# One more buffer in each ring of a scan unit, and two of its inputs made a unit earlier

## What is computed

```python
x = L0(x)   # layernorm, two state-space scans (one over the reversed sequence), gate, residual
x = L1(x)   # layernorm, token gather, conv, one state-space scan, gate, residual
x = L2(x)   # softmax attention, 16 heads
x = L3(x)   # linear attention, 8 heads
```

```python
delta = softplus(dlt @ Wdt.T + bdt)
dA  = exp(delta[..., None] * A)                     # B, S, E, N
dBu = delta[..., None] * Bm[:, :, None, :] * u[..., None]
h = dA_t * h + dBu_t                                # step by step over the 256 tokens
y = einsum('ben,bn->be', h, C_t)
```

## Time and profile before

| what | us |
|---|---|
| median of 3 runs | 3707.52 |
| lowest, highest | 3702.73, 3718.88 |
| span of the profiled execution | 3709.0 |

### The profile page before, as it was taken

How to read it: one execution, slowest core, us unless ns; L and a number is a source line. 1 busy time by engine, 2 the same in 40 slices (tenths; PEclk the granted TensorE clock), 3 DMA queues, 4 the chain that set the end, 5 groups by cost and what they waited for, 6 DMA issues and landing times.

```text
span 3709.0 us, 64650 instructions
## 1 busy us (share of the span) xinstructions
PE 3242.9 (87%) x22078; PEld 2674.0 (72%) x22078; DVE 2851.3 (77%) x3590; ACT 2921.7 (79%) x6624; POOL 2833.8 (76%) x3087
## 2 busy tenths in 40 slices
PE   6677788899999999999999999899989999897876
PEld 2556667787777878787877778787877777675643
DVE  1568778889797979798887979798888979793621
ACT  1658878888889898888888898988988898873522
POOL 0578989888898889888888888888888889780500
PEclk8899999999999999999999999999999999997866
DMA  4112222222122222212221222212221222220100
GB/s 170 59 51 82 80 66 65 85 65 88 61 87 63 83 63 80 74 59 89 65 87 58 82 69 79 71 60 89 63 88 60 87 61 78 60 69 19 44 2 10
DMA packets 140951, 257.08 MB, mean 69 GB/s; under 512 B 15921, under 2 KB 33329, under 8 KB 140225
## 3 DMA queue, kind: packets, MB, share of 16 engines
q1 hardware_dynamic: 140626, 252.95, 22.0%
HBM read 233.16 MB, written 5.05 MB: 64 GB/s over the span
## 4 chain that ended last, share of the span: by engine, by line
PE 48%; ACT 22%; DVE 11%; POOL 6%; issue 6%; DMA 0%; SPq 0%; POOLq 0%; DVEq 0%; ACTq 0%
PE ps_b L574 10%; PE ps_y L602 9%; ACT decay L639 8%; POOL g L693 5%; DVE hst L678 4%; PE ps_x L771 4%; ACT dbut L649 4%; PE ps_x L1276 3%; PE ps_x L765 3%; PE ps_v L765 3%; PE ps_x L1301 2%; PE ps_v L771 2%; PE ps_x L774 2%; PE ps_v L790 2%; ACT pT L1355 2%
## 5 line engine op out<-in xcount | busy, mean ns | idle before, releaser
L693 POOL TENSOR_TENSOR g<-hst,c_bc 128x512 f32<-128x512 f32 x1536 | 1976.1, 1287 | 482.2 <-PE ps_y L602 349.0
L678 DVE TENSOR_TENSOR_SCAN hst<-decay,ps_b 128x512 f32<-128x512 f32 x1536 | 1832.7, 1211 | 399.0 <-PE ps_b L574 231.8
L639 ACT ACTIVATE decay<-delta,acoef 128x256 f32<-128x256 f32 x3072 | 1378.4, 498 | 56.8 <-DVE hst L678 56.4
L574 PE MATMUL ps_b<-ident,dbut 128*128 128x128 f32 x6144 | 951.9, 278 | 241.4 <-DVE hst L678 110.3
L658 POOL TENSOR_TENSOR dbut<-dut,bcm 128x256 f32<-128x256 f32 x1536 | 972.4, 633 | 190.7 <-ACT dut L864 190.7
L602 PE MATMUL ps_y<-ident,g 128*128 128x128 f32 x6144 | 943.0, 276 | 20.8 <-ACT u L965 17.4
L574 PEld LDWEIGHTS ps_b<-ident,dbut 128*128 128x128 f32 x6144 | 708.0, 143 | 333.3 <-ACT dbut L649 165.1
L602 PEld LDWEIGHTS ps_y<-ident,g 128*128 128x128 f32 x6144 | 734.6, 142 | 147.4 <-issue 55.5
L649 ACT ACTIVATE dbut<-dut,bcm 128x256 f32<-128x256 f32 x1536 | 767.4, 500 | 22.0 <-PE ps_b L574 18.8
L1355 ACT ACTIVATE pT<-ps_x 128x1024 f32<-128x1024 f32 x128 | 129.5, 1012 | 74.5 <-PE ps_x L1311 64.3
L1301 PE MATMUL ps_x<-qT,kT 18*128 18x256 f32 x1024 | 159.6, 433 | 16.7 <-ACT pT L1355 15.6
(11 more groups left out here) (192 smaller groups left out, 4080.3 us busy)
## 6 DMA issues: line engine op xcount, KB each, us to landing
c_bc<-c_rows SPq DMA_DIRECT2D x768, 256.0 KB, 3.2
rows_bc<-mod_rows SPq DMA_DIRECT2D x16, 384.0 KB, 4.4
ada_w<-in_ada_w_dram SPq DMA_DIRECT2D x1, 5120.0 KB
weights<-in_weights_dram SPq DMA_DIRECT2D x1, 4832.0 KB, 34.8
x<-in_x_dram SPq DMA_DIRECT2D x16, 256.0 KB, 3.8
x0p<-x SPq DMA_DIRECT2D x16, 256.0 KB, 2.3
xr<-x SPq DMA_DIRECT2D x16, 256.0 KB, 2.3
x<-x SPq DMA_DIRECT2D x16, 256.0 KB, 3.6
```

The lines of the kernel that those rows point to most:

```text
L574: last = nc.tensor.matmul(ps_b[:, u % 2, e * T + t * P:e * T + (t + 1) * P], dbut[:, u % NDBU, t, e * P:(e + 1) * P], ident[:, :], is_tran ...
L639: last = nc.scalar.activation(decay[:, u % (DA_AHEAD + 2), e, :], delta[s][:, eb, :], ACT.Exp, scale=acoef[:, s, eb, n:n + 1])
L678: nc.vector.tensor_tensor_scan(line(hst[:, u % NHST, :, :].rearrange("p e t -> p (e t)")), line(decay[:, u % (DA_AHEAD + 2), :, :].rearran ...
L693: nc.gpsimd.tensor_tensor(g[:, u % NG, :, :], hst[:, u % NHST, :, :], c_bc[:, k % NCB * CHUNK + n % CHUNK, :].unsqueeze(1) .broadcast_to([ ...
```

## The change

Six constants and one argument change. dbut goes from 4 to 5 buffers, hst and g from 3 to 4, decay (DA_AHEAD + 2) from 4 to 5. The dBu halves are issued 4 units ahead of the scan in place of 3, the decays 3 ahead in place of 2. The two banks of ps_b, the lead of spread_b (B_AHEAD = 2) and LAG stay. The room in SBUF comes from the scratch for DMAs whose descriptors software writes, which is set to 1024 bytes.

```diff
@@ -27,7 +27,7 @@
 B_AHEAD = 2
-DA_AHEAD = 2
+DA_AHEAD = 3
 LAG = 2
@@ -52,9 +52,9 @@
-NDBU, NHST, NG, NPT = 4, 3, 3, 2
-A_AHEAD = 3
-P_AHEAD = 3
+NDBU, NHST, NG, NPT = 5, 4, 4, 2
+A_AHEAD = 4
+P_AHEAD = 4
@@ -1740,7 +1740,7 @@
-    nc = _bacc.Bacc("TRN2", target_bir_lowering=False, num_devices=1)
+    nc = _bacc.Bacc("TRN2", target_bir_lowering=False, num_devices=1, dynamic_dma_scratch_size=1024)
```

## The result

| | before | changed |
|---|---|---|
| median, us | 3704.59 (20 runs) | 3688.49 (20 runs) |
| lowest to highest, us | 3684.66 to 3726.45 | 3680.93 to 3696.97 |
| span of the profiled execution, us | 3709.0 | 3681.1 |

The ratio is 0.996, with a 95% interval of 0.9945 to 0.9975: 0.4% faster, or 16 us between the medians. The forecast was 39.5 us. The measured time lies within the half per cent that the prediction called no change. (One correction to the text ahead of the prediction: line 1058 stands at tick 5 of a period, not at tick 2.)

What follows compares the result with a forecast made beforehand. Four engines near their limits, PE nearest, were taken as the bound. One third of 124 us of removable waits, 41 us, less 1.5 us for starts, gave 39.5 us: 3668 us, range 3626 to 3713.

Steps and rivals of the forecast that it cites:

- What bounds the kernel: Steady part: PE 93% busy, ACT 88%, DVE and POOL 86% each; four engines near their limits, the last one changing.
- dBu and decay leads: Longer leads make PE's dbut and DVE's decay waits nearly vanish; upper bound for dbut 80.7 us of PE's idle time.
- the yield of one third of 124 us: Of 80.7 + 43 us of removable waits, one third, 41 us, shortens the run, by ACT's and POOL's chain share.
- hst ring: Fourth buffer lets the scan run one unit further ahead of POOL; DVE's 54.9 us for g vanish; upper bound 43 us.
- g ring, taken at nothing: Fourth g buffer lets POOL run one unit further ahead of PE's sums; nothing taken, at most 53.0 us in first stretch.
- It waits later instead: Reason for giving the g ring nothing: where POOL is behind nobody, running further ahead only moves its wait.
- Starts and scratch: Extra work at three starts delays the first scan 0.50 us each, 1.5 us in all; the smaller scratch costs nothing.
- The rival "nothing gained", 0.25: Moved waits turn into others, through ACT's throughput and ps_b; about 3700 us; chance of no visible gain 0.25.
- The rule of the Trainium skill: Improving the most-contended engine improves a kernel; the change takes work off no engine, so time stays at 3707 us.
- The rival "slower: DVE locked out", 0.08: POOL without gaps holds the port pair shared with DVE; two more long stalls per period, 80 us; about 3745 us; chance 0.08.
- Its test: Lockout sign: mean of line 751, 1058 or 882 rises by a microsecond or more and POOL's hst waits grow.
- More than the sum, by the clock: Fewer waits avert clock falls and the yield is two thirds: 82 us and more, about 3625 us; larger gain's chance 0.12.

Runs made afterwards that it cites:

- e10_before_yield: Kernel before, plus two POOL waits per period: ahead of unit 4's g for the column copy, unit 6's for the norm's scaling; 3671.22 us, 0.9933 of before.
- e9_leads_yield: Changed kernel with hst and g back at 3 buffers, plus POOL waits per period ahead of the g of units 4 and 6; 3672.24 us, 0.9948 of before.
- e1_leads: Changed kernel with hst and g back at 3 buffers, so only the dbut and decay leads and rings; 3732.61 us, 1.0101 of before.
- e5_hst_only: Kernel before with hst at 4 buffers and the small scratch; 3659.41 us, 0.9915 of before.
- e11_leads_hst_yield: Changed kernel with g back at 3 buffers, plus POOL waits per period ahead of the g of units 4 and 6; 3656.19 us, 0.9894 of before.
- e6_g_only: Kernel before with g at 4 buffers and the small scratch; 3679.83 us, 0.9958 of before.
- e7_after_yield: Changed kernel plus two POOL waits per period: ahead of unit 4's g for the column copy, unit 6's for the norm's scaling; 3634.86 us, 0.985 of before.
- e2_rings: Changed kernel with dbut and decay leads and rings taken back, hst and g at 4; 3679.12 us, 0.9945 of before.
- e12_best: Changed kernel without line 1058's copy, POOL waiting ahead of the g of units 6 and 81 for two norms' scalings; 3617.77 us, 0.9791 of before.

## Why the prediction was wrong in size

- **What bounds the kernel.** Four engines near their limits held. What I read too quickly is that an engine which shares something with another sets more than its own waits: POOL's idle time was useful to DVE.
- **dBu and decay leads.** The mechanism was right, as far as the waits go (80.7 to 20.0 us on PE; 92.7 to 18.4 on DVE). The step that failed is the yield of one third of 124 us. For the leads it is nothing: e10_before_yield and e9_leads_yield measure the same. Without gaps it is minus 1.0% (e1_leads).
- **hst ring.** Here the yield was too low, if anything. The upper bound was 43 us and a third of it 14; e5_hst_only gained 0.85% (31 us), e11_leads_hst_yield over e9_leads_yield half a per cent.
- **g ring, taken at nothing.** The second failed step. It is worth some 0.4% (e6_g_only, which has the small scratch too, and from e11_leads_hst_yield to e7_after_yield), and it lengthens the copy. "It waits later instead" overlooked that POOL, when it runs ahead, keeps PE's and DVE's next waits small, and that its waits were DVE's openings.
- **Starts and scratch.** The first scan waits 5.4 us for its decay, where it waited 5.0: 0.4 us for the 0.50 of the sum. No run has the scratch alone. It is small in e2_rings, e5_hst_only and e6_g_only as well, so what these gain over before is the rings' and the scratch's together; that the scratch is worth 0 is not shown.
- **The rival "nothing gained", 0.25.** It had the time (3700 us; the median is 3688.49) but not the mechanism. It said that waits would come back for ps_b; DVE's rose from 231.8 to 306.2 us, as said. But with gaps in both kernels the change gains 0.8%, so the moved waits are not all turned into others.
- **The rule of the Trainium skill**, page Perfetto Trace Analysis (Identifying Performance Opportunities), that one gains by improving the most-contended engine, gave no change, and the result is close. Yet e12_best won 2.1% at nearly the same work of every engine (PE 3213.1 us busy against 3242.9), so the rule did not say why.
- **The rival "slower: DVE locked out", 0.08.** This is what happened, and its sign was outweighed. I priced two more long stalls in each period at 80 us. There was one in place of the short one, 2.7 us longer on average (4461 less 1765 ns, 43 us in all), while the norm's fell by 31 us. Its test, a mean of line 1058 up by more than 1 us, came true. The argument against it, that the end of a stall does not move because DVE arrives earlier, was the third failed step. The end is POOL's next gap. In the timeline of the changed kernel that came only when the scanned units had run out, and DVE had arrived with three of them outstanding.
- **More than the sum, by the clock.** This did not come. The mean granted clock is 0.951 in both profiled executions, but before's was one of its slower ones. Over all runs whose clock is on record it is 0.949 with the change (20 runs) and 0.953 before (52 runs, timed beside the experiments). Before's own runs are faster at a higher clock: 3679.72 us at 0.957, 3720.02 us at 0.947, and a straight line through all 52 gives 2.8 us for 0.001. By that, as an estimate, the lower clock goes with some 11 us of the missing gain. Whether the clock is a cause or follows from PE's stalls isn't shown. It fell to 0.66 behind the new stall and was 1.00 in e7_after_yield at the same place, from 1880 to 1890 us.

- **How the shortfall divides.** Forecast were 39.5 us, measured 16. With the same gaps in both kernels it is 31 us, by the ratios, so the lockout that the change made worse holds about two thirds of the missing 23.5 us, with an uncertainty of more than half of that. The rest is what the leads did not yield (27 us were forecast for them), less what the hst ring yielded above its 14 us and the g ring above nothing.

What stays open: why the copy gets through after one instruction of POOL in some periods and after several in others, what the scratch does alone, and what part the clock has in the difference.

## What to carry to other kernels

When a deeper ring removes waits, ask which engine lived in those waits. Look in the trace for short instructions whose duration differs between periods (here 0.16 to 5.94 us): that is a wait which no list of waits shows. Try each ring and each lead by itself, and where two engines exclude each other, put one short wait on the long-running one at the unit where the other needs its turn.

## What the runs showed of the hardware

A DVE copy of 128x4 elements takes 0.16 us with POOL idle (at 3347.23 us before), and up to 5.94 us with POOL at work (at 470.70 us in the changed kernel). It is not held for one instruction of POOL but, in the timeline of the changed kernel, while six in a row ran, g and dbut in turn. In e7_after_yield a gap of 0.16 us was enough. Of the lock the Trainium skill's page SBUF — State Buffer (SBUF: two separate sides) says that one engine's instruction holds the port pair as a whole while the other blocks; the trace agrees with the block, and shows that the waiting engine isn't sure of its turn at the next instruction. The scan itself (1207 to 1211 ns in every one of before, changed and e7_after_yield) is not affected by POOL's work, nor is POOL's g much (1287 to 1300 ns). The granted clock falls behind a single idle stretch of PE of 4.76 us: it was 1.00 from 1905 to 1910 us and 0.66 on average from 1910 to 1915 us, so PE ran at the lower of its levels, 1.2 of 2.4 GHz, for a part of these 5 us.
